# One core, an AdaLN block with a selective scan and top-2 experts: rows of C by DMA instead of by matmul

## What is computed

```
h   = layernorm(x) * (1 + ca) + sa                      # modulation by a small matmul of silu(c)
x_dbl = h @ W_x.T                                       # 64 rows dt_raw, 16 rows B, 16 rows C
dt  = softplus(dt_raw @ W_dt.T + b_dt)
A_bar = exp(dt * A) ;  dB_u = (dt * h) * B              # for each channel and each of 16 states
s_t = A_bar_t * s_(t-1) + dB_u_t                        # recurrence over the 1024 tokens
y   = sum over 16 states of s * C  + h * D
x   = x + ga * y
h   = layernorm(x) * (1 + cb) + sb
x   = x + gb * (sum of the two best of 8 experts of h, with softmax gates)
```

## Time and profile before

| | us |
|---|---|
| three runs | 1138.73, 1139.85, 1143.65 (median 1139.85) |
| the profiled execution, its own time | 1137.84 |
| its span, first to last instruction | 1135.8 |
| busy: VectorE, GpSimd, TensorE, ScalarE | 990.9, 934.9, 917.4, 781.4 |
| DMA, mean busy share of the 16 engines | 44.8% on the one queue |

### The profile page before, as it was taken

How to read it: one execution, slowest core, us unless ns; L and a number is a source line. 1 busy time by engine, 2 the same in 40 slices (tenths; PEclk the granted TensorE clock), 3 DMA queues, 4 the chain that set the end, 5 groups by cost and what they waited for, 6 DMA issues and landing times. The chain is left out here.

```text
span 1135.8 us, 14810 instructions
## 1 busy us (share of the span) xinstructions
PE 917.4 (81%) x4187; PEld 581.1 (51%) x4203; DVE 990.9 (87%) x1294; ACT 781.4 (69%) x1618; POOL 934.9 (82%) x373
## 2 busy tenths in 40 slices
PE   6336544699788988899879988899879988699998
PEld 4002111266555655456545656465536655366886
DVE  2799999999999999999999999999999999994200
ACT  5686789588967898588866897688867595442100
POOL 2376667699989999699988999799979998897553
PEclk9556665599999998899899998999889999899999
DMA  4925241627155534546174635556271716411222
GB/s 124 237 62 140 59 111 38 168 84 194 54 136 159 148 103 102 160 108 171 47 169 125 162 83 130 135 138 151 57 188 48 195 47 150 120 34 62 69 85 71
DMA packets 89793, 131.28 MB, mean 116 GB/s; under 512 B 13280, under 2 KB 73256, under 8 KB 89200
## 3 DMA queue, kind: packets, MB, share of 16 engines
q1 hardware_dynamic: 89712, 130.34, 44.8%
HBM read 54.50 MB, written 8.65 MB: 56 GB/s over the span
## 5 line engine op out<-in xcount | busy, mean ns | idle before, releaser
L1104 POOL TENSOR_TENSOR h<-h,Cr 128x2048 f32<-128x2048 f32 (+1 forms) x131 | 582.0, 4444 | 36.4 <-DVE h L989 13.1
L676 PE MATMUL ps<-xg,we 128*128 128x256 f32 x2048 | 492.5, 397 | 6.4 <-POOL xg L1138 3.6
L676 PEld LDWEIGHTS ps<-xg,we 128*128 128x128 f32 x2048 | 399.8, 199 | 88.6 <-issue 28.4
L724 ACT ACTIVATE av<-dd,An 128x512 f32<-128x512 f32 x512 | 351.0, 714 | 70.6 <-DVE h L989 64.4
L1138 POOL TENSOR_TENSOR xg<-h2T,gbc 128x1024 f32<-128x1024 f32 x128 | 303.3, 2372 | 59.0 <-PE ps L676 42.2
L976 DVE TENSOR_TENSOR ps<-ps,dd 128x512 f32<-128x512 f32 x512 | 326.4, 684 | 3.3 <-DMA dd<-src 2.8
L989 DVE TENSOR_TENSOR_SCAN h<-av,kept,ps 128x512 f32<-128x512 f32 x256 | 313.5, 1264 | 3.1 <-PE ps L569 2.5
L989 DVE TENSOR_TENSOR_SCAN h<-av,ps 128x512 f32<-128x512 f32 x256 | 298.0, 1204 | 11.1 <-PE ps L569 8.3
L569 PE MATMUL ps<-h,gam 128*32 128x512 f32 x1024 | 157.1, 741 | 53.6 <-POOL h L1104 25.2
L569 PEld LDWEIGHTS ps<-h,gam 128*32 128x32 f32 x1024 | 31.1, 124 | 134.4 <-issue 99.9
L1011 DVE TENSOR_TENSOR X<-ps,X 128x512 f32<-128x512 f32 x32 | 21.7, 679 | 64.1 <-PE ps L647 64.1
(11 more groups left out here) (105 smaller groups left out, 812.1 us busy)
## 6 DMA issues: line engine op xcount, KB each, us to landing
dd<-src SPq DMA_DIRECT2D x480, 128.0 KB, 2.4
gbc<-gates SPq DMA_DIRECT2D x128, 256.0 KB, 3.4
X<-in_x SPq DMA_DIRECT2D x8, 1024.0 KB, 6.9
out<-X SPq DMA_DIRECT2D x32, 256.0 KB, 3.5
XN<-in_x SPq DMA_DIRECT2D x7, 1024.0 KB, 7.3
dd<-src SPq DMA_DIRECT2D x16, 256.0 KB, 5.0
we<-in_We SPq DMA_DIRECT2D x2, 1024.0 KB, 10.8
XN<-in_x SPq DMA_DIRECT2D x2, 512.0 KB, 4.5
```

The source lines that it names most:

```text
L676: e = pe.matmul(bk[:, m * 256:(m + 1) * 256], we[:, hf, 2 * ep + e2, m * P:(m + 1) * P], xg[:, i % XG, e2, hf], start=(ep == e2 == m == hf ...
L724: act.activation(av[:, u % AS], step_of(u, 0), ACT.Exp, scale=An[:, 0, i:i + 1]).then_inc(s_a, 1)
L1104: pool.tensor_tensor(hu, hu, Cr[:, q:q + 1].to_broadcast([P, n, CH]), ALU.mult).then_inc(s_ch, n)
```

## The change

The 16 rows of C are taken from the same product with W_x, where they stand as rows 80 to 95. ScalarE's copy into `rows` is widened from 64 to 96 partitions. A new step `cw` on SP's queue writes these 16 rows of a half (32 KB) to DRAM, and four steps `cr` read them back, each four rows with every row repeated to 32 partitions (256 KB), into one of now eight places of Cr. The C matmuls and ScalarE's copies of C are gone, and GpSimd's products wait for the transfer's semaphore. The gate rows in `rows` and the bias rows move to partitions 96 to 103. The table AT is replaced as a whole, so the order of nearly every engine moves a little; the diff shows a line or two of it.

```
--- before.py
+++ after.py
@@ -23,28 +23,28 @@
...
-          ldx=32.62, gam=43.66, dl0=21.77, dl1=32.96, dls=1.81, rdl=1.02, sp=1.37, dt=8.06, C=24.84, CS=3.7, rC=0.8,
...
+AT = dict(cw=3.83, cwH=14.08, exp=-0.92, mul=-0.32, scan=0.28, ch=6.84, Bs=-2.05, y=7.72, stat0=-4.29,
...
@@ -99,8 +99,9 @@
             put(s + AT["ddu" + hd] + AT["ddus" + hd] * j, "ddu", 2 * b + c, j)
         for q in range(NQ):
             s = t + AT["C" + hd] + AT["CS" + hd] * q + T // 2 * c
-            put(s, "C", b, c, q)
-            put(s + AT["rC" + hd], "read", "C", b, c, q)
+            if q == 0:
+                put(s - AT["cw" + hd], "cw", b, c)
+            put(s, "cr", b, c, q)
 
 
 def beside(b, t, put):
@@ -207,7 +208,7 @@
     return u >= TOTAL - 4
 
 
-SHARED = ("md", "xT", "wx", "dl", "C", "lg", "lT", "gT", "o")
+SHARED = ("md", "xT", "wx", "dl", "lg", "lT", "gT", "o")
 
 
 def unit(u):
@@ -251,7 +252,7 @@
 
     def ring(self, s):
 
-        if s[0] == "md" or s in (("C", 0, 0, 0), ("C", 0, 0, 1)):
+        if s[0] == "md":
             return self.HEAD
         if s[:3] == ("xT", 0, 0) or s[:2] == ("wx", 0) or s[:3] == ("dl", 0, 0):
             return self.HEAD
@@ -265,6 +266,7 @@
     plan = schedule()
     bank = Bank(plan)
     gd = nc.dram_tensor("gates", (2, E, L), F32, kind="Internal").ap()
+    cd = nc.dram_tensor("crows", (2, N, CH), F32, kind="Internal").ap()
     with ExitStack() as ctx:
         def sb(name, shape, dt=F32):
             return ctx.enter_context(nc.sbuf_tensor(name, shape, dt))
@@ -310,9 +312,9 @@
         src = sb("src", [P, 2, L])
         dd = sb("dd", [P, NJ, 2, L])
         rows = sb("rows", [P, L])
-        dtr, gT = rows[0:R], rows[R:R + E]
+        dtr, gT = rows[0:96], rows[96:96 + E]
         S = sb("S", [P, 2, L], F32R)
-        Cr = sb("Cr", [P, NQ, CH])
+        Cr = sb("Cr", [P, 2 * NQ, CH])
         av = sb("av", [P, AS, CH])
         h = sb("h", [P, HS, L])
         XM = sb("XM", [P, 4, D])
@@ -322,7 +324,7 @@
         selE = h[:, 0]
         wx = sb("wx", [P, 2, P])
         wrow = sb("wrow", [P, D])
-        wdt, beb = wrow[0:R], wrow[R:R + E]
+        wdt, beb = wrow[0:R], wrow[96:96 + E]
         we = sb("we", [P, 2, E, D])
         wm = h[:, 5:8].rearrange("p n l -> p (n l)").rearrange("p (k m) -> p k m", k=2)
         cc = sb("cc", [P, 3, 2, NB])
@@ -365,6 +367,7 @@
                                                 for n in ("s_mean", "s_sq", "s_ln", "s_rd", "s_rs", "s_xh"))
         s_ga, s_gam = sem("s_ga"), sem("s_gam")
         s_dtr, s_hi = sem("s_dtr"), sem("s_hi")
+        s_cw, s_cr = [sem(f"s_cw{i}") for i in range(2)], [sem(f"s_cr{i}") for i in range(2 * NQ)]
         s_dt, s_dtu = sem("s_dt"), sem("s_dtu")
         s_br, s_a, s_bm, s_scan, s_ch, s_y, s_z = (sem(n) for n in
                                                    ("s_br", "s_a", "s_bm", "s_scan", "s_ch", "s_y", "s_z"))
@@ -482,6 +485,20 @@
                     if b >= 2:
                         sp.wait_ge(s_o[b % 2], 64 * (b // 2))
                     sp.dma_start(X2[:, b % 2], x[b].rearrange("(k p) d -> p k d", p=P)).then_inc(s_x2[b % 2], 16)
+                elif s[0] == "cw":
+                    _, b, c = s
+                    sp.wait_ge(s_dtr, 2 * b + c + 1)
+                    if b:
+                        for q in range(NQ):
+                            sp.wait_ge(s_cr[4 * c + q], 16 * b)
+                    sp.dma_start(cd[c], rows[80:96, c * CH:(c + 1) * CH]).then_inc(s_cw[c], 16)
+                elif s[0] == "cr":
+                    _, b, c, q = s
+                    n = 8 * b + 4 * c + q
+                    sp.wait_ge(s_cw[c], 16 * (b + 1))
+                    if b:
+                        sp.wait_ge(s_ch, 8 * (n - 7))
+                    sp.dma_start(Cr[:, 4 * c + q], cd[c, 4 * q:4 * q + 4].unsqueeze(1).to_broadcast([4, 32, CH])).then_inc(s_cr[4 * c + q], 16)
                 elif s[0] == "ddt":
                     _, H, j = s
                     positive(sp, *divmod(H, 2))
@@ -613,15 +630,7 @@
                 elif s[0] == "dl":
                     _, b, c, hf = s
                     pe.wait_ge(s_dtr, 2 * b + c + 1)
-                    e = pe.matmul(bk, wdt[:, hf * P:(hf + 1) * P], dtr[:, c * CH:(c + 1) * CH], start=True, stop=True)
-                elif s[0] == "C":
-                    _, b, c, q = s
-                    if q == 0:
-                        if b == 0:
-                            pe.wait_ge(s_sel, 1)
-                        emptied(pe, ("wx", b, c))
-                    e = pe.matmul(bk, sel[R:P, NQ + q],
-                                  S[R:P, b % 2, c * CH:(c + 1) * CH], start=True, stop=True)
+                    e = pe.matmul(bk, wdt[:, hf * P:(hf + 1) * P], dtr[0:R, c * CH:(c + 1) * CH], start=True, stop=True)
                 elif s[0] == "lg":
                     b, halves = s[1], s[2:] or (0, 1)
                     for c in halves:
@@ -745,10 +754,10 @@
                     done(act, s)
                     if b:
                         done(act, ("dl", b - 1, c, 1))
-                    act.activation(dtr[:, cs], mb(s)[0:R], ACT.Copy).then_inc(s_dtr, 1)
+                        act.wait_ge(s_cw[c], 16 * b)
+                    act.activation(dtr[:, cs], mb(s)[0:96], ACT.Copy).then_inc(s_dtr, 1)
                     if b >= 2:
                         act.wait_ge(s_br, 8 * (b - 1) - 4 + 4 * c)
-                        done(act, ("C", b - 2, c, NQ - 1))
                     act.activation(S[R:P, b % 2, cs], mb(s)[R:P], ACT.Copy).then_inc(s_hi, 1)
                 elif s[0] == "dl":
                     _, b, c, hf = s
@@ -771,13 +780,6 @@
                         act.wait_ge(s_dtu, H + 1)
                     done(act, s)
                     release(act.activation(src[:, 0, cs], mb(s), ACT.Identity, bias=bd[:, hf:hf + 1]), s)
-                elif s[0] == "C":
-                    _, b, c, q = s
-                    n = 8 * b + 4 * c + q
-                    if n >= 4:
-                        act.wait_ge(s_ch, 8 * (n - 3))
-                    done(act, s)
-                    release(act.activation(Cr[:, q], mb(s), ACT.Copy), s)
                 elif s[0] == "lg":
                     done(act, s)
                     k0, k1 = blocks(s)
@@ -1094,14 +1096,14 @@
                 b, c, q, _, _ = unit(u)
                 n = 1 if alone(u) else 4
                 pool.wait_ge(s_scan, u + 1)
-                emptied(pool, ("C", b, c, q))
+                pool.wait_ge(s_cr[4 * c + q], 16 * (b + 1))
                 at = u % (2 * HS) + 1
                 hu = h[:].rearrange("p s (a l) -> p (s a) l", a=2)[:, at - n:at]
                 if c == 0:
                     i = u % 32 - 3
                     pool.tensor_copy(kept[:, i:i + 4].unsqueeze(2), hu[:, :, CH - 1:CH]).then_inc(s_kept, 1)
                     pool.wait_ge(s_kept, 8 * b + i // 4 + 1)
-                pool.tensor_tensor(hu, hu, Cr[:, q:q + 1].to_broadcast([P, n, CH]), ALU.mult).then_inc(s_ch, n)
+                pool.tensor_tensor(hu, hu, Cr[:, 4 * c + q:4 * c + q + 1].to_broadcast([P, n, CH]), ALU.mult).then_inc(s_ch, n)
 
             for s in plan:
                 if s[0] == "ch":
```

60 lines of the change are left out of this document (27 added, 33 removed).

## The result

The changed kernel takes 1155.74 us (median of 4 runs, 1153.92 to 1160.78) against 1139.29 (4 runs, 1138.70 to 1143.65): **1.43% slower**, ratio 1.0143, 95% interval 1.0101 to 1.0185. The profiled execution took 1156.73 us, its span is 1155.0 against 1135.8.

The account below looks back on a forecast made before the run. VectorE was taken to bound the kernel, busy 97.5% of the middle. The profiled 1137.84 us, +6 for the head's broadcasts and −4 for shorter waits, gave 1139.84, on the median 1142 us; range 1132 to 1153.

Parts of the forecast that it names:

- Frame: Whole kernel: head, middle bound by VectorE, tail; delay of dd or ga in the head reaches the end one for one.
- dd 2 us later: Head: x of batch 1 now goes ahead of dd, making dd 1 to 3 us later, taken as 2.
- Broadcasts in the head, +6: Head: broadcasts queued ahead of ga make it later, 2.8 to 5.6 us by issue times; 6 us taken, up to +12.
- rival 2: Broadcasts occupy four of sixteen DMA engines, 3.3 us each: +9 in the head, +1 from the middle, 1150 us; chance 0.29.
- Removed matmuls and copies, 0 directly and −4 indirectly: Middle: removed TensorE and ScalarE work is hidden by VectorE, worth 0; shorter VectorE waits give −4 us, ends 0 and 13.
- the 14.9 us of waits: Middle: VectorE's waits for TensorE's sums of y and ScalarE's copy into S, 14.9 us that could vanish.
- Rival 3: TensorE's sums come later, from order and less granted clock: a further us per batch, +6 head, about 1153 us; chance 0.08.
- Steady-state broadcasts 0: Middle: four broadcast issues ahead of dd's turnover, 2.2 us, fit within 4.6 us of slack, so cost 0.
- Statistics and first products, 0: Head: batch 1's statistics between the first exps and GpSimd's second dt product behind gam each cost 0.
- Tail 0±1.5: Tail: GpSimd's 23 expert products and TensorE's 23 expert groups remain in both orders, so 0, ends ±1.5 us.

Follow-up runs that it names:

- e3: Changed kernel with the time table of the kernel before and each C row written four times, so broadcasts start with 16 rows: 1151.0 us, ratio 1.0085.
- e6: e3 with its head mended: first broadcast ahead of dd, ga ahead of the last two broadcasts, x of batch 1 and weights: 1147.0 us, ratio 1.0054.
- e4: Changed kernel with ga's 16 small transfers right behind dd, ahead of the broadcasts and the weights: 1156.0 us, ratio 1.0123.
- e1: Changed kernel, new table kept, each C row written to DRAM four times so broadcasts start with 16 rows: 1144.7 us, ratio 1.0044.
- e5: e3 with the 64 C matmuls back at their old places, ScalarE reading one column of each: 1141.0 us, ratio 0.9999.
- e10: e6 with the 64 C matmuls back at their old places, ScalarE reading one column of each: 1143.8 us, ratio 1.0016.
- e7: Kernel before with ga's 16 transfers ahead of the expert weights, nothing else: 1139.6 us, ratio 0.9980.
- e12: e10 with each of the 64 C matmuls over 8 columns instead of 512: 1138.1 us, ratio 0.9995.

## Why the prediction was wrong

The forecast was 1142 us, the range 1132 to 1153; 1155.74 lies outside. By its steps:

- **Frame: right, but for one thing.** Head, middle and tail are the three stretches. That what the head loses goes to the end one for one holds only roughly: F 5.7 us earlier gave 4.1 us (e3 to e6), 3.7 us earlier gave nothing (e4).
- **dd 2 us later: near.** It was 1.0 at its start and 1.3 at its end; x of batch 1 went at 24.73, not at 21.95, since TensorE took longer for the same matmuls and transposes ahead of it (last section).
- **Broadcasts in the head, +6: the term that failed, mis-sized.** It charged a broadcast between the price of 256 KB elsewhere and four times it, near the lower end, but it runs on four engines: 102 GB/s, share 0.26. The head measured +11.0, where rival 2 had +9 with ends of 6.5 and 12. Its 3.3 us for one broadcast on four engines were 2.6. (A slip of 0.3 us in its sum changes nothing: it took 1.24 us for an issue in a full queue, where 18.68/16 is 1.17.) The step "I take 6 us, just above the first range, as this pattern starts with 4 rows while every transfer priced here starts with 16 or more" named the right feature and drew too little from it. The rule of the Trainium skill, "DMA: Bandwidth & Descriptors", section "Why a DMA increments its semaphore by 16 and not by 1", that the outermost dimensions decide, agrees with the trace (0.26, and 1.02 in e1) and deserved more than 0.29.
- **Removed matmuls and copies, 0 directly and −4 indirectly: wrong in sign as a whole.** The S wait did go. But the step that "indirectly it can shorten the 14.9 us of waits" looked only at work that ends late because other work stands ahead of it, not at what the removed matmuls held in place. The middle measured +7.7. For the old table the runs price the matmuls: without them the kernel is 10 us slower (e3 against e5), in the mended head 3.2 us (e6 against e10). The copies' part of the −4 seems to be there: with the matmuls back and the copies still gone, M is 928.4 (e5) against 933.2 before, in one profile each. For the new table no run puts the matmuls back, so how much of the 7.7 us is theirs stays open; the trace has the waits for x, gs, sums and an exp and the longer shift in its place. Rival 3 named the lower clock as a possibility with 0.08 and put it at the sums; with the old table it is at the routing's transposes and logits, and half of the wait there.
- **Steady-state broadcasts 0: right as far as the profiles tell.** M is the same with four engines or sixteen (941.0, 941.3; 939.9, 938.4), and VectorE waits for no transfer in the middle.
- **Statistics and first products, 0: harmless only because ga covered it.** VectorE's first multiplication came at 38.47 instead of 31.11. In the new order VectorE's correction of the second half's S stands ahead of it, and that S came 5.2 us later, with TensorE's product (32.63 instead of 27.43, last section):

```profile
37.74 0.70 DVE L999 TENSOR_TENSOR S<-ps,S 32x512 fp32r<-32x512 f32 x1 [2.61 <-ACT S L761]
```

  In e1 ga ends at 64.24, 2.9 us later than before, and VectorE waits only 1.06 us for the sums at unit 16: without that wait it would be there at 69.80, against 65.39 before (66.97−1.58).
- **Tail 0±1.5: right**, +0.5. (With the old table and the broadcasts, e3, it is 110.8, 2.6 more than before.)
- **Rival 2 came nearest**, with 1150: its head was 2 short, its middle 6.7.

What stays open: what made the middle of the changed kernel 7.7 us longer, beyond the waits named, and with it whether the new table adds anything of its own in the middle of the changed kernel (e1 and e3 differ by 2.9 us in M, within what single profiles can tell, but by 6.3 us in the medians, the new table being the faster one), and why GpSimd's product comes later and a matmul of 8 columns is enough to prevent it.

## What to carry to other kernels

Before a broadcast replaces compute, look at the first dimension of the source: four rows repeated to 32 partitions each occupied four DMA engines for 2.6 us here, and large transfers behind them in the queue took longer to issue (10.11 us for the weights against 1.63); writing the rows four times so that the source starts with 16 bought 11 us, 7 of them seen in the head of the trace. Small transfers on which the first sums depend belong ahead of large ones that nobody needs yet (0.2% in the kernel before, e7). And work removed from an engine that is not the bound can cost time: here the engine then idled longer and made the next step that others wait for at a lower clock, while a copy ahead of it came later behind a third engine, and the bound engine paid for both. Read the row of that step, its wait and its duration, not the engine's busy share.

## What the runs showed that was not expected

- 64 matmuls that nobody reads made a kernel 10 us faster (1151.0 to 1141.0; 3.2 us with the mended head), and over 8 columns did no worse (1138.1).
- One program has several rhythms. In e12's profile batches with a 2.2 us wait stand among others without one; in e10 executions cluster near 1135 and near 1144 us, the mean granted clock going with them. A single profile can lie 9 us beside the median (e10, 1134.35 against 1143.8).
- In the head TensorE ran the same four matmuls of dt in 1.95 us in one execution and in 3.75 in another, with a granted clock of 1.00 shown in both; the second modulation comes 5 us later then. Before, and likewise in e3, they took 1.95 from 18.98 us on; after, and likewise in e5, whose table is the old one, the timeline of TensorE has

```profile
19.06 3.75 PE L633 MATMUL ps<-rows,wrow 64*128 64x512 f32 x4 [0.78 <-ACT rows L758]
```
